# Three attention layers on one core: key weights in halves, totals from the exponentials, and one block of scores moved

## What is computed

```python
def _mha(q_in, k_in, v_in, wq, bq, wk, bk, wv, bv, wo, bo, padding_mask, causal):
    q = (q_in @ wq + bq).reshape(Bq, Sq, H, DK).transpose(0, 2, 1, 3)
    k = (k_in @ wk + bk).reshape(Bq, Sk, H, DK).transpose(0, 2, 1, 3)
    v = (v_in @ wv + bv).reshape(Bq, Sk, H, DV).transpose(0, 2, 1, 3)
    scores = jnp.einsum('bhqd,bhkd->bhqk', q, k)
    ...
    attn = jax.nn.softmax(scores / math.sqrt(DK), axis=-1)
    out = jnp.einsum('bhqk,bhkd->bhqd', attn, v)
    return out.transpose(0, 2, 1, 3).reshape(Bq, Sq, H * DV) @ wo + bo
...
sa = _mha(input, input, input, ..., causal=True)
x = _layer_norm(sa + residual, ln1_g, ln1_b)
ca = _mha(x, encoder_output, encoder_output, ..., causal=False)
x = _layer_norm(ca + residual, ln2_g, ln2_b)
h = jax.nn.relu(x @ ffn_w1 + ffn_b1)
x = _layer_norm(h @ ffn_w2 + ffn_b2 + residual, ln3_g, ln3_b)
...
q = rope(q); k = rope(k)          # third block
attn = jax.nn.softmax(jnp.where(m, q @ k^T / sqrt(64), -1e9), axis=-1)
y = layer_norm(x + (attn @ v) @ Wo)
```

## Time and profile before

| | |
|---|---|
| Time, median of 3 | 525.77 us (523.55 to 526.3) |
| The profiled execution: time | 527.22 us |
| The profiled execution: span of the trace | 525.3 us, mean granted TensorE clock 0.992 |
| TensorE busy | 506.3 us (96%) |
| VectorE busy | 436.8 us (83%) |
| ScalarE busy | 367.6 us (70%) |
| GpSimd busy | 295.5 us (56%) |
| DMA | 12.74 MB, 21 GB/s over the span |

### The profile page before, as it was taken

One profiled execution on the slowest core, in us unless ns is written; L12 is line 12 of the kernel. 1 busy time (PEld: TensorE's weight loads), 2 busy tenths in 40 slices (PEclk: granted clock), 3 DMA queues, 4 the chain that ended last, 5 costly groups with the idle time before them and its releaser, 6 DMA issues.

```text
span 525.3 us, 23789 instructions
## 1 busy us (share of the span) xinstructions
PE 506.3 (96%) x10336; PEld 470.6 (90%) x10336; DVE 436.8 (83%) x776; ACT 367.6 (70%) x1002; POOL 295.5 (56%) x581
## 2 busy tenths in 40 slices
PE   6989999999999999999999999999999999999986
PEld 6789999999999999999999998889999999999885
DVE  4898999977889877877878788999889888888873
ACT  5676675765876766767567686678687887888761
POOL 2553534534437445343536335888777887887825
PEclk9999999999999999999999999999999999999989
DMA  7910000000012010000000000000000000000000
GB/s 236 316 69 4 4 2 2 2 4 2 3 42 82 2 43 3 2 3 1 4 2 2 2 2 2 3 3 4 2 8 9 14 8 9 13 8 9 7 9 21
DMA packets 10838, 12.74 MB, mean 24 GB/s; under 512 B 752, under 2 KB 8432, under 8 KB 10736
## 3 DMA queue, kind: packets, MB, share of 16 engines
q1 hardware_dynamic: 10736, 11.24, 7.0%
HBM read 10.18 MB, written 1.05 MB: 21 GB/s over the span
## 4 chain that ended last, share of the span: by engine, by line
PE 78%; ACT 12%; DVE 4%; issue 2%; POOL 1%; DMA 1%; SPq 0%; POOLq 0%; DVEq 0%
PE ps_p L677 14%; PE ps_p L507 7%; PE ps_p L648 7%; PE ps_p L509 7%; PE ps_p L508 7%; ACT kT L762 6%; PE ps_a L562 5%; PE ps_a L584 5%; PE ps_p L637 4%; PE ps_a L544 4%; PE ps_p L639 4%; PE ps_p L638 4%; PE ps_p L584 4%; PE ps_p L698 2%; ACT probs L800 2%; PE ps_a L555 2%
## 5 line engine op out<-in xcount | busy, mean ns | idle before, releaser
L1179 POOL TENSOR_TENSOR small<-mv,epsilon 128x1 f32<-128x1 f32 x48 | 9.6, 199 | 170.1 <-DVE mv L936 170.1
L677 PE MATMUL ps_p<-wo,headsT 128*128 128x128 f32 x768 | 95.3, 278 | 2.0 <-DVE headsT L915 0.9
L677 PEld LDWEIGHTS ps_p<-wo,headsT 128*128 128x128 f32 x768 | 91.4, 193 | 5.2 <-issue 1.9
L907 DVE TENSOR_TENSOR turn<-ps_p,rope 128x1024 f32<-128x1024 f32 x64 | 76.0, 1221 | 11.6 <-PE ps_p L509 10.2
L754 ACT ACTIVATE vv<-ps_p 128x512 f32<-128x512 f32 x96 | 57.1, 619 | 27.3 <-PE ps_p L639 23.8
L507 PE MATMUL ps_p<-xT_hi,wq_hi 128*128 128x256 f32 x192 | 58.6, 305 | 1.1 <-issue 0.8
L790 ACT ACTIVATE probs<-ps_a,top 128x64 f32<-128x64 f32 x256 | 56.0, 353 | 4.4 <-DVE top L980 3.4
L1010 DVE TENSOR_REDUCE total<-probs 128x16 f32<-128x1024 f32 x48 | 58.2, 1212 | 0.2
L762 ACT ACTIVATE qT<-ps_p,columns 128x256 f32<-128x256 f32 x126 | 49.4, 494 | 10.1 <-PE ps_p L509 10.1
L508 PE MATMUL ps_p<-xT_lo,wq_hi 128*128 128x256 f32 x192 | 54.2, 282 | 0.0
L509 PE MATMUL ps_p<-xT_hi,wq_lo 128*128 128x256 f32 x192 | 54.1, 282 | 0.0
(11 more groups left out here) (143 smaller groups left out, 1429.2 us busy)
## 6 DMA issues: line engine op xcount, KB each, us to landing
out<-y_out SPq DMA_DIRECT2D x16, 64.0 KB, 2.8
X<-in_x SPq DMA_DIRECT2D x1, 768.0 KB, 7.6
across<-in_across SPq DMA_DIRECT2D x1, 704.0 KB, 9.5
wq_raw<-in_L_xattn_sa_wq SPq DMA_DIRECT2D x2, 256.0 KB, 2.9
wk_raw<-in_L_xattn_sa_wk SPq DMA_DIRECT2D x1, 512.0 KB, 5.9
wv_raw<-in_L_xattn_sa_wv SPq DMA_DIRECT2D x1, 512.0 KB, 8.2
wo<-in_L_xattn_sa_wo SPq DMA_DIRECT2D x1, 512.0 KB, 8.2
wo<-in_L_xattn_ca_wo SPq DMA_DIRECT2D x1, 512.0 KB, 8.7
```

The source lines that it names most:

```text
L677: last = mm(bank[:, 0:E], headsT[:, p, :, :].rearrange("r b q -> r (b q)"), wo[:, layer % 2, p, :], start=(p == 0), stop=(p == PAIRS - 1))
L907: ins = V.tensor_tensor(turn[:, j % 2, :, :].rearrange("d a (h b t) -> d a h b t", h=2, t=S), bank[:, None, :].broadcast_to([128, 2, 512]) ...
```

## The change

Five edits are made together. (1) The first layer's key weights are loaded in two halves like the query weights, with one DMA issue more on SP; ScalarE and VectorE split them in halves of 512 columns, and the key products K0 and K1 wait for the first half alone, K2 for the second. (2) `keep_clock(4)` is called twice more: after the last query piece of step -2, and before scores(0). (3) In units 30 to 45 each exponential also writes its row total (`accum_out`), and VectorE's sum L1010 is left out for these units. (4) In the odd steps 9 to 19 the fourth key piece (K3) is emptied by VectorE instead of ScalarE, in VectorE's queue behind the two normalisations and ahead of the weights and of Y. (5) In step 46 scores(47) stand behind the two P fills, ahead of Y(44).

```diff
+def key_takers(u):
+    if u < 0:
+        return "AAAD" if u == FIRST else "ADAD"
+    return "AAAD" if u % 2 and 8 < u < UNITS + 5 else "AAAA"
...
-            project.append((name + "r", j, "D") if rotary(u) else (name, j, ("AAAD" if u == FIRST else "ADAD" if u < 0 else "AAAA")[j]))
+            project.append((name + "r", j, "D") if rotary(u) else (name, j, key_takers(u)[j]))
...
         elif name == "sum":
-            steps += [("sum",), ("recip",)] + ([] if split_heads(u) else [("rinv",)])
+            steps += ([] if by_head(u) else [("sum",)]) + [("recip",)] + ([] if split_heads(u) else [("rinv",)])
...
     if u % 2:
-        return head + [("sum", 0), ("norm", 0, u), ("norm", 1, u)] + weights + fout + ffn + stat + fgain + those("Y")
+        return head + [("sum", 0), ("norm", 0, u), ("norm", 1, u)] + those("K") + weights + fout + ffn + stat + fgain + those("Y")
...
-            return layer + (2 if n == 0 else 1)
+            return layer + (2 if n < 2 else 1)
...
-            sp.dma_start(w_raw[0][:, first], weight(0, "q")[:, first]).then_inc(half_loaded, 16)
-            sp.dma_start(w_raw[0][:, second], weight(0, "q")[:, second]).then_inc(w_loaded[0], 16)
-            sp.dma_start(w_raw[1][:, :], weight(0, "k")).then_inc(w_loaded[1], 16)
+            for n in range(2):
+                sp.dma_start(w_raw[n][:, first], weight(0, "qk"[n])[:, first]).then_inc(half_loaded[n], 16)
+                sp.dma_start(w_raw[n][:, second], weight(0, "qk"[n])[:, second]).then_inc(w_loaded[n], 16)
...
-                            pe.wait_ge(w_ready[n_w], parts_ready(g * CU // UNITS, n_w) - (1 if name == "Q" and g == 0 else 0))
-                    if (name, j, g) == ("Q", 2, 0):
-                        pe.wait_ge(w_ready[0], 2)
+                            pe.wait_ge(w_ready[n_w], parts_ready(g * CU // UNITS, n_w) - (1 if g == 0 else 0))
+                    if (j, g) == (2, 0):
+                        pe.wait_ge(w_ready[n_w], 2)
...
+                if u == 0:
+                    keep_clock(4)
                 if attends(u) and u != N - 1:
                     scores(u)
...
-                    if (u, name, j) == (N - 2, "P", 0):
+                    if (u, name, j) == (N - 2, "Y", 0):
                         scores(N - 1)
...
-                    if u == FIRST and name == "T":
+                    if u == FIRST and (name == "T" or (name, j) == ("Q", 3)):
                         keep_clock(4)
...
                         ins = nc.scalar.activation(probs[:, u % 2, n, :], ps_a[:, bank, 64 * k:64 * k + 64], ACT.Exp,
-                                                   bias=top[:, at:at + 1], scale=scale)
+                                                   bias=top[:, at:at + 1], scale=scale, accum_out=total[:, n:n + 1])
...
-                V.tensor_reduce(total[:, :], probs[:, u % 2, :, :], AX_X, ALU.add).then_inc(dve_step, 1)
-                dve.wait_ge(dve_step, VSTEP.at(u, "sum"))
+                if not by_head(u):
+                    V.tensor_reduce(total[:, :], probs[:, u % 2, :, :], AX_X, ALU.add).then_inc(dve_step, 1)
+                    dve.wait_ge(dve_step, VSTEP.at(u, "sum"))
```

More of the change, by code:

```diff
@@ L361, in build @@
         second_x_loaded = sem("second_x_loaded")
-        half_loaded = sem("half_loaded")
+        half_loaded = [sem(f"half_{n}_loaded") for n in "qk"]
         x_loaded = sem("x_loaded")
@@ L813, in split_high @@
                 layer, n = new_weights(u, after_input)
-                if (layer, n) == (0, 0):
-                    act.wait_ge(half_loaded, 16)
-                    nc.scalar.activation(w_hi[0][:, 0:H * D // 2], w_raw[0][:, 0:H * D // 2], ACT.Copy).then_inc(w_hi_ready[0], 1)
-                    act.wait_ge(w_loaded[0], 16)
-                    nc.scalar.activation(w_hi[0][:, H * D // 2:H * D], w_raw[0][:, H * D // 2:H * D], ACT.Copy)\
-                      .then_inc(w_hi_ready[0], 1)
+                if layer == 0 and n < 2:
+                    act.wait_ge(half_loaded[n], 16)
+                    nc.scalar.activation(w_hi[n][:, 0:H * D // 2], w_raw[n][:, 0:H * D // 2], ACT.Copy).then_inc(w_hi_ready[n], 1)
+                    act.wait_ge(w_loaded[n], 16)
+                    nc.scalar.activation(w_hi[n][:, H * D // 2:H * D], w_raw[n][:, H * D // 2:H * D], ACT.Copy)\
+                      .then_inc(w_hi_ready[n], 1)
                     return
@@ L1031, in split_rest @@
                 layer, n = new_weights(u, after_input)
-                if (layer, n) == (0, 0):
+                if layer == 0 and n < 2:
                     for k in range(2):
                         half = slice(H * D // 2 * k, H * D // 2 * (k + 1))
-                        dve.wait_ge(w_hi_ready[0], k + 1)
-                        V.tensor_tensor(w_lo[0][:, half], w_raw[0][:, half], w_hi[0][:, half].bitcast(F32), ALU.subtract)\
-                         .then_inc(w_ready[0], 1)
+                        dve.wait_ge(w_hi_ready[n], k + 1)
+                        V.tensor_tensor(w_lo[n][:, half], w_raw[n][:, half], w_hi[n][:, half].bitcast(F32), ALU.subtract)\
+                         .then_inc(w_ready[n], 1)
                     return
```

## The result

The change made the kernel slower: 530.28 us median (530.1 to 533.62, 4 runs) against 524.84 us (523.55 to 526.3, 4 runs). The ratio is 1.0124, 95% interval 1.0081 to 1.0168. I had predicted 522.9 and a range up to 530.0, and the time lies above it. The profiled execution of the changed kernel took 530.34 us (span 528.5), 3.1 more than the profiled execution of before.

A forecast was written before the change was run, and what follows sets the result against it. TensorE, busy 96%, was taken as the bound, with idle time at both ends and a lower clock behind pauses. Terms -2.4 + 0.2 + 0.8 - 1.5 = -2.9 took the median 525.77 to 522.9 us; range 520.5 to 530.0.

The forecast's parts named there:

- Part 1: At the start, key weights loaded and split in halves plus unread products: -2.4 us, bounds -1.0 and -2.6.
- the earlier start: K0, the first key product, starts at 9.6 instead of 10.55 because the weights come in halves: -0.95 us.
- the bank of Q0: If the first half lands earlier, K0 waits for ScalarE to empty this bank, at about 9.6; same date either way.
- The clock term: At the start, fifteen K matmuls run at the upper clock level instead of granted 0.50: -1.5 us.
- The price of the products: Four unread products before scores(0) lie in its 1.06 us wait for kT, costing only what they outlast it by.
- Part 2: K3 emptied by VectorE in six odd units: the wait of scores changes hands, +0.2 us, bounds -1.1 and +0.6.
- x 6: One odd unit's K3 ends no sooner on VectorE, +0.03 us, multiplied for the six units.
- Part 3: Row totals from the exponentials in units 30 to 45, VectorE's sums removed: +0.8 us, bounds 0 and +12.
- The price a: Added ScalarE time per exponential that also writes a total: 0.08 us chosen, bounded by 0 and 0.148 or 0.20.
- the cover of 1.5 us a unit: ScalarE's wait before the transposed weights in each late unit hides the totals' 1.3 us; break-even 0.094 per exponential.
- Rival C: ScalarE becomes the bound in units 32 to 45: slower, 534.1 us at 0.148 per exponential, 546 at 0.20; chance 0.22.
- Part 4: Last scores behind both transposes, stall partly gone and Y(44) at full clock: -1.5 us, bounds -2.4 and +1.2.

## Why the prediction was wrong

**Part 1, predicted -2.4.** Of the two terms, the earlier start (-0.95) was right in mechanism: the wait for wk_lo is gone in every trace with halves, and in one of them the bank of Q0 took over, as I had foreseen, with 0.97 us. What it brings at scores(0) was 0.4 on the mean of the traces, all of it the first trace's, so no gain is shown. The clock term (-1.5) took one execution's slow stretch for a property of the kernel. The fall of the clock at 11.8 us stands in that trace alone; the four other traces without halves have none, two of them behind waits of 1.11 and 2.05 us for the same wk_lo. The slow products of the changed kernel, seventeen among the queries, are of another kind, a late first rise of the clock, for which the prediction had no term. One execution could not carry the term. It was also a little too large for its own rows: fifteen products at 0.21 instead of 0.12 us are 1.4. The base itself was that execution, 527.22, 2.4 to 3.7 above the medians; I noted a difference of 1.4 and carried the terms over whole.

**The price of the products, predicted none.** The step that failed is that the products "would cost only what they outlast it by", the wait in which they stand: I counted their time in the pause, not that 32 instructions more move everything behind them in TensorE's program. This cost 2.3 us at scores(33) (12.39 against 10.07), some 330 us after the edit. The stall among the query products of that step was in the list of TensorE's waits of the kernel before:

```profile
PE ps_p L507 <- issue: 0.8, 1, 0.8
```

The prediction does not mention it; I did not see that it could be pushed into the scores. It is the largest single miss, and no rival had it.

**Part 2, predicted +0.2, measured +2.2 in the trace.** The steps ahead of step 15 did as computed: 139.97 to 140.11 for the fifteen units up to scores(15), against 139.94 and 139.95. The step that failed is "x 6": I priced one step and multiplied. Step 15 has other work beside it on GpSimd, and its normalising pair took 3.45 us in the trace of before already. One look at all six would have shown it. That a wait of this length can bring the lower clock, 1.5 us more in one trace of four, was not in the bounds either.

**Part 3, predicted +0.8, measured +1.0 to +1.6 in the late units and 2.4 in the time of that part alone.** The 2.4 hold 0.9 of the stall in scores(34), of which it is open whether it belongs to the totals. The price a = 0.08 against 0.09 measured was nearly right, and so was the cover of 1.5 us a unit: of 2 x 16 x 0.09 = 2.9 us added in two units 0.3 came through, so 1.3 a unit was hidden. The term was mis-sized in what is left over: I charged 0.1 in every second unit, and every second unit lost 0.25 (10.51 against 10.26), in the step behind the one with the input eviction, the other units 0.07, and the step from scores(35) to scores(36) 0.37 (14.30 against 13.93). Rival C had the engine right and the size far too high: it was priced at 0.148 and 0.20, and 0.09 was measured. The rule that the Trainium skill ("VectorE: DVE Perf Modes", Two Vector instructions with no wait between them) gives for VectorE, that writing out the accumulator is a second instruction, holds for ScalarE in this trace; its price, though, was the small one, 0.09 and not a whole exponential.

**Part 4, predicted -1.5, measured -0.5.** The order of things was right: P waited 0.80 for V's banks, the stall went, Y(44) ran at full pace (508.59 to 510.57). The whole stall went, where I had left 0.8 of it. The term was sized with 0.9 + 0.8 us of lower clock that the kernel before shows in one of its two traces.

**The sum.** The parts measured alone or undone give +2.2 (key piece in step 15), +2.2 to +3.2 (products), +1.0 to +2.4 (totals), 0 to -0.4 (halves) and -0.5 (late scores): between +4.5 and +7.3. The parts are not all clean of each other, since stalls and falls of the clock come in some executions only. All together measured +5.4 against its own runs of before and up to +6.7 against the later ones. Nothing large is left over, but a part of 1 us could hide in that width.

## What to carry to other kernels

Price a repeated edit at every place where it lands, against what other engines do there, not at one and times six. Instructions added anywhere move every later one in that engine's program. In this kernel, a wait that the profile calls "issue" and that stood at the same instruction in two traces was such a fixed place: what was added ahead of it decided which instructions it hit, and short, dense products were where it cost most. And before a term rests on a slow stretch of one execution, look whether a second trace, or the median of the runs, contains it.

## What the runs showed of the hardware

An exponential with a total is two instructions on ScalarE in the trace, and adds 0.09 us to its pace at 64 columns. A VectorE instruction on 128x512 fp32 with both inputs in SBUF took 2.84 us instead of 0.69 beside a GpSimd subtraction of 2.9 us. TensorE's query products at the start came 0.21 us apart instead of 0.12 for none to twenty of them, differently in each of the fourteen traces, and then rose to full pace (at 8.0 us in the kernel with halves alone, at 9.8 in the changed kernel). In the eight traces with more than one slow product the clock records begin within 0.1 us of that rise, and for the time ahead of them the windows read 1.00: at the very start the pace has to be read from the distance between products. A TensorE stall without a releaser stood behind 6222 products in thirteen of fourteen traces (behind 6223 in the other), with 0, 4 or 16 pairs of weight load and product added 330 us earlier.
